# A four-layer sequence kernel on one core: the first attention of the next row in one stretch with the FFN of this row and the experts of the row before, without barriers between rows

## Time and profile before

| | us |
|---|---|
| median of 3 runs | 1578.21 |
| lowest and highest | 1576.48, 1590.58 |
| the profiled execution, its own time | 1577.19 |
| its span, first to last instruction | 1575.4 |
| busy in the span: TensorE | 1289.6 (82%) |
| VectorE | 851.7 (54%) |
| ScalarE | 666.1 (42%) |
| POOL | 107.2 (7%) |
| mean granted TensorE clock | 0.891 |

### The profile page before, as it was taken

The page is one execution under the profiler, slowest core; times in us unless marked ns, Lnnn a source line. Parts: engine busy times, 40 slices in busy tenths (PEclk is TensorE's granted clock), DMA queues, the critical chain, the costliest instruction groups (busy, mean ns, idle before and its releaser), DMA issues.

```text
span 1575.4 us, 19401 instructions
## 1 busy us (share of the span) xinstructions
PE 1289.6 (82%) x7257; PEld 643.8 (41%) x7257; DVE 851.7 (54%) x1816; ACT 666.1 (42%) x1407; POOL 107.2 (7%) x250
## 2 busy tenths in 40 slices
PE   2499458788898998788799899878789899878888
PEld 1122133445122564344322365444422267344556
DVE  6587446333785467433677365624578456633222
ACT  1067323352376442343166542254157643235232
POOL 4000001020000000020000000003000000000000
PEclk6599769799799999889699999889989999879989
DMA  7400000030000000030000000030000000000000
GB/s 149 111 2 2 8 0 1 21 41 2 1 2 2 1 7 1 1 61 9 2 2 2 1 7 1 1 61 2 7 1 2 1 1 1 1 1 1 8 1 8
DMA packets 31731, 21.04 MB, mean 13 GB/s; under 512 B 12873, under 2 KB 29329, under 8 KB 31633
## 3 DMA queue, kind: packets, MB, share of 16 engines
q1 hardware_dynamic: 31632, 19.75, 6.3%
HBM read 14.96 MB, written 4.19 MB: 12 GB/s over the span
## 4 chain that ended last, share of the span: by engine, by line
PE 64%; DVE 18%; ACT 7%; SPq 4%; issue 3%; DMA 2%; POOL 0%; DVEq 0%; POOLq 0%; PEldq 0%; ACTq 0%; another core or an unknown queue 0%
PE ps L1210 8%; PE ps L1142 8%; PE ps L1152 7%; DVE mx L726 6%; PE ps L1177 6%; PE ps L1291 6%; PE ps L1312 5%; PE ps L1185 5%; PE ps L1281 4%; ACT ps L1038 3%; PE ps L1324 3%; DVE mx L843 2%; DVE SH L817 2%; PE ps L1384 2%; ACT PROB L981 2%
## 5 line engine op out<-in xcount | busy, mean ns | idle before, releaser
L981 ACT ACTIVATE PROB<-ps 128x512 f32<-128x512 f32 x512 | 272.4, 606 | 284.0 <-PE ps L1177 283.9
L726 DVE TENSOR_REDUCE mx<-ps 128x1 f32<-128x512 f32 x512 | 318.7, 683 | 86.0 <-PE ps L1185 85.9
L1185 PE MATMUL ps<-KPAD,SH 128*128 128x512 bf16 x512 | 193.8, 431 | 54.9 <-SPq L352 35.0
L1038 ACT ACTIVATE ps<-ps,mx 128x128 f32<-128x128 f32 (+3 forms) x256 | 127.1, 497 | 252.6 <-DVE mx L843 252.6
L1312 PE MATMUL ps<-KPAD,SH 64*128 64x384 f32 (+3 forms) x512 | 171.4, 530 | 58.4 <-ACT ps L1038 50.2
L843 DVE TENSOR_REDUCE mx<-ps 128x1 f32<-128x128 f32 (+3 forms) x256 | 113.6, 486 | 189.8 <-PE ps L1315 189.8
L1177 PE MATMUL ps<-SH,KPAD 128*128 128x512 bf16 x512 | 163.3, 395 | 15.2 <-ACT PROB L981 9.9
L1291 PE MATMUL ps<-SH,KPAD 64*128 64x256 f32 (+3 forms) x512 | 139.5, 536 | 40.1 <-DMA m1row<-mrow 22.9
L1210 PE MATMUL ps<-PROB,v 128*32 128x512 f32 x1024 | 138.0, 614 | 6.8 <-ACT SH L972 4.7
L959 ACT ACTIVATE KPAD<-ps,b_sb 128x512 f32<-128x512 f32 x128 | 87.9, 687 | 126.8 <-PE ps L1142 126.4
L1312 PEld LDWEIGHTS ps<-KPAD,SH 64*128 64x128 f32 x512 | 79.9, 219 | 117.7 <-ACT ps L1038 98.2
(11 more groups left out here) (175 smaller groups left out, 1361.9 us busy)
## 6 DMA issues: line engine op xcount, KB each, us to landing
SH<-qk_parts SPq DMA_DIRECT2D x48, 128.0 KB, 6.4
qk_parts<-SH SPq DMA_DIRECT2D x8, 384.0 KB, 2.9
w_sb<-in_L_ffn_W_dram SPq DMA_DIRECT2D x1, 2048.0 KB
XN<-in_L_attn_x_dram SPq DMA_DIRECT2D x4, 256.0 KB, 2.9
out_dram<-XP SPq DMA_DIRECT2D x4, 256.0 KB, 2.3
wq_sb<-in_L_attn_Wq_dram SPq DMA_DIRECT2D x1, 512.0 KB, 5.4
rope_sb<-in_rope_dram SPq DMA_DIRECT2D x1, 512.0 KB
wo_sb<-in_L_attn_Wo_dram SPq DMA_DIRECT2D x1, 512.0 KB
```

The lines of the kernel that those rows point to most:

```text
L726: dve.tensor_reduce(mx[:, ga % 2, r % 16:r % 16 + 1], ps[:, 3 + r % 3, :], AX, ALU.max, negate=True).then_inc(max0_done, 1)
L981: act.activation(prob0[:, n % 2, c, k], ps[:, q % 3, :], ACT.Exp, scale=float(HD0) ** -0.5).then_inc(exp0_done, 1)
L1038: act.activation(tile, tile, ACT.Exp, bias=mx[:, (s + 1) % 2, col:col + 1], accum_out=lsum[:, (s + 1) % 2, 0, col:col + 1]).then_inc(sum1_ ...
L1185: pe.matmul(ps[:, 3 + r % 3, :], qst[:, a // 8, P * qt:P * (qt + 1)], kpad[:, a // 8, j, :], start=True, stop=True).then_inc(a0_ready, 1)
```

## The change

The loop over rows becomes an unrolled alternation of two stretches, the same on every engine: `overlap(-1)`, `attention1(-1)`, `overlap(0)`, `attention1(0)`, ..., `attention1(3)`, `overlap(4)`.

- `overlap(r)` goes through the 88 slots with first attention of row r + 1, the first FFN of row r (`ffn_stream`) and the experts of row r - 1 (`experts_stream`), whichever exist. `overlap(-1)` has first attention alone, `overlap(0)` no experts, `overlap(3)` no first attention, `overlap(4)` the experts of row 3 alone.
- `attention1(r)` is second attention of row r. In it stand the outputs, sum, norm and block scales of first attention of row r + 1, and turning, projecting and splitting x of row r + 2. `attention1(-1)` has only these.
- Semaphores count on through the rows; barriers and clearing are gone. Each row's output leaves by its own wait.
- Terms lie in 32-row strips: 24 rows of terms and 3 of maxima for each of the four head halves of a group (`M_ROW` is 24). A score or maximum uses one strip of `kst` and `qst`, `kpad` and its masked copies are gone. The terms are laid out on the way to DRAM: 12 stores for 2, 8 loads for 12. The row of maxima takes three transfers a group for one. POOL's per-row memsets of `kst` and `qst` are gone.
- PSUM: scores of first attention have 2 banks for 3 (0, 1), maxima and their turned rows share 2 (2, 3), values bank 4, experts 5 and 6, FFN 6 and 7. Experts have one hidden buffer, up products use banks 5 and 6, down products bank 6. In second attention maxima have 4 banks (2 to 5), scores one pair (0, 1).
- Rotary sums, the last four passes of both quantisations and the bias of the output are on POOL. Square roots (`std_b`, and of the RMS norm) stand between the exponentials of second attention (slots (0, 4) and (1, 4)) and of first attention (7, 2).

The core of the diff; the streams of VectorE and ScalarE follow the same tables of slots:

```diff
...
-A1_BANK = (4, 5, 7)
 
...
+A_LEAD = 13
+STEPS = [(s, c) for s in range(-4, 18) for c in range(4)]
...
+GATE_UP = {(-4, 0): 0, (-4, 2): 1, (-3, 0): 2, (-3, 2): 3}
+SILU = {(-4, 1): 0, (-4, 3): 1, (-3, 1): 2, (-3, 3): 3}
+HID_TURN = {(3, 0): 0, (4, 0): 1, (5, 0): 2, (6, 0): 3}
+HID_KEEP = {(3, 1): 0, (4, 1): 1, (5, 1): 2, (6, 1): 3}
+DOWN = {(3, 2): 0, (4, 2): 1, (5, 2): 2, (6, 2): 3}
+DOWN_KEEP = {(3, 3): 0, (4, 3): 1, (5, 3): 2, (6, 3): 3}
+O0_TURN = {(9, 0): 0, (9, 2): 1, (10, 0): 2, (10, 2): 3, (11, 3): 4, (13, 3): 5, (15, 3): 6, (17, 3): 7}
+O0_OUT = {(2 * g + 3, 0): g for g in range(NG)}
+UP = {(2 * e - 1, f): (e, f) for e in range(NE) for f in range(4)}
+OUT = {(2 * e, t): (e, t) for e in range(NE) for t in range(NT)}
+COMBINE = {(2 * e + 1, 0): e for e in range(NE)}
...
+def qk_banks(i):
+    return (0, 1) if i % 2 == 0 else (6, 7)
+
+
+def a1_bank(i):
+    return 2 + i % 4
...
+            def store_parts(k):
+                if k:
+                    sp.wait_ge(terms_in, 16 * 2 * HF * k)
+                for c, part in enumerate((Q_PART, K_PART)):
+                    sp.wait_ge(parts_ready, 2 * k + c + 1)
                     for t in range(NTERM):
-                        src = parts_dram[1 - c, part[t]].rearrange("(g r) n -> r g n", g=NG)
-                        sp.dma_start(dst[16 * t:16 * t + 16], src).then_inc(terms_in, 16)
...
+                        dst = terms_dram[c, t].rearrange("d j g n -> (j g) d n")
+                        sp.dma_start(dst, split[:, c, part[t]]).then_inc(parts_out, 16)
+                sp.wait_ge(parts_out, 16 * 2 * NTERM * (k + 1))
+
+            def load_terms(k):
+                if k:
+                    sp.wait_ge(av0_done, 16 * k)
+                for c, dst in ((1, kst), (0, qst)):
+                    for j in range(HF):
+                        src = terms_dram[c].rearrange("t d j g n -> j (t d) g n")[j]
+                        sp.dma_start(dst[32 * j:32 * j + M_ROW], src).then_inc(terms_in, 16)
...
+                    sp.wait_ge(slot0_free, SLOTS * k + ROW_SLOT[g] + 1)
+                    for i in range(3):
+                        sp.dma_start(qst[M_ROW + i::32, g, :], mrow0[16 * i:16 * i + 16, :]).then_inc(max0_in, 16)
+                    sp.wait_ge(max0_in, 48 * (NG * k + g + 1))
...
-                sp.wait_ge(row_ended, len(row_opened))
-                sp.sem_clear(row_ended)
-                clear(late)
-                for opened in row_opened:
-                    sp.sem_inc(opened, 1)
-
-            def body(row, first, last):
...
+            def rope_sum(r, i):
+                pool.wait_ge(rope_ready, 24 * r + 2 * (i + 1))
+                d = QK_ORDER[i]
+                dst = qT[:, d] if d < 8 else k1[:, d - 8]
+                pool.tensor_tensor(dst, ropeT[:, i % 2, 0], ropeT[:, i % 2, 1], ALU.add).then_inc(qk_ready, 1)
+
+            def quantise(a, c, n, done):
+
+                nb = n // QB
+                blk = lambda t: t.rearrange("p (b q) -> p b q", q=QB)
+                wide = lambda t: t.rearrange("p (b a) -> p b a", a=1).broadcast_to([P, nb, QB])
+                step(pool.tensor_scalar(c, c, 1.0, 1.5 * 2.0 ** 22, ALU.max, ALU.mult)); settle()
+                step(pool.tensor_tensor(a, a, c, ALU.add)); settle()
+                yield
+                step(pool.tensor_tensor(a, a, c, ALU.subtract)); settle()
+                pool.tensor_tensor(blk(a), blk(a), wide(q_sc[:, 0, 0:nb]), ALU.mult).then_inc(done, 1)
+                yield
...
+            def overlap(r):
+                k = r + 1
+                hidden = 0 <= r < BATCH
+                if hidden:
+                    pool.wait_ge(hs_ready, r + 1)
+                    rounds = quantise(ha, hc, 1408, hq_ready)
...
+                    if hidden and g < 2:
+                        next(rounds)
+                    if k < BATCH:
+                        max_parts0(k, g)
...
+                    if g == 2 and k < BATCH:
+                        pool.wait_ge(xs_ready, k + 1)
+                        for _ in quantise(XQ[:, :], ZB[:, :, :].rearrange("p t n -> p (t n)"), T, xq_ready):
+                            pass
+                    if g == 3 and nx < BATCH:
+                        split_next(nx, 0)
+                        split_next(nx, 1)
...
+                if (s, c) in UP:
+                    e, f = UP[s, c]
+                    if (e, f) == (0, 0):
+                        pe.wait_ge(ohT_ready, i + 1)
+                    if (e, f) == (0, 1) and i + 1 < BATCH:
+                        pe.wait_ge(hid_done, NT * (i + 2))
+                    if f == 1 and e:
+                        pe.wait_ge(comb_done, NT * (NE * i + e))
+                    if f >= 2 or e:
+                        pe.wait_ge(relu_done, 32 * i + 4 * e + f - 1)
+                    pe.matmul(ps[:, 5 + f % 2, :], w1_sb[:, e, P * f:P * (f + 1)], xnT[:, :], start=True, stop=True).then_inc(up_ready, 1)
+                if (s, c) in OUT:
+                    e, t = OUT[s, c]
+                    if t == 0:
+                        pe.wait_ge(relu_done, 32 * i + 4 * (e + 1))
+                    for f in range(4):
+                        ins = pe.matmul(ps[:, 6, P * t:P * (t + 1)], hE[:, f, P * t:P * (t + 1)], w2_sb[:, e, f, :],
+                                        start=(f == 0), stop=(f == 3))
+                    if t == NT - 1:
+                        ins.then_inc(down1, 1)
...
+                    if t == 0:
+                        pe.wait_ge(xT_ready, 2 * r + 1)
+                    else:
+                        pe.wait_ge(hid_done, NT * r + t)
+                    for u in range(2):
+                        ins = pe.matmul(ps[:, 6 + u, 0:FF0], xT[:, P * t:P * (t + 1)], wgT[:, u, :], start=True, stop=True)
+                    ins.then_inc(gu_ready, 1)
...
+            def overlap(r):
+                k, i = r + 1, r - 1
+                for s, c in STEPS:
+                    if k < BATCH:
+                        if 0 <= s < 16:
+                            g = s // 2
+                            if c == 0 and s % 2 == 0:
+                                pe.wait_ge(max0_in, 48 * (NG * k + g + 1))
+                            for q in (8 * s + 2 * c, 8 * s + 2 * c + 1):
+                                j, kt = q % 4, 2 * (s % 2) + q % 8 // 4
+                                rows = slice(32 * j, 32 * j + M_ROW + 3)
+                                if 128 * k + q >= 2:
+                                    pe.wait_ge(exp0_done, 128 * k + q - 1)
+                                pe.matmul(ps[:, q % 2, :], kst[rows, g, P * kt:P * (kt + 1)], qst[rows, g, :],
                                           start=True, stop=True).then_inc(s0_ready, 1)
-                        if 0 <= a < HF * 2 * NG:
-                            for u in range(2):
-                                r = 2 * a + u
-                                j, qt = r % 16 // 4, r % 4
-                                if r >= 3:
-                                    pe.wait_ge(max0_done, r - 2)
-                                pe.matmul(ps[:, 3 + r % 3, :], qst[:, a // 8, P * qt:P * (qt + 1)], kpad[:, a // 8, j, :],
-                                               start=True, stop=True).then_inc(a0_ready, 1)
...
+                        for n in maxima_at(s, c):
+                            j, qt, at = n % 4, n % 16 // 4, SLOTS * k + MAX_SLOT[n]
+                            rows = slice(32 * j, 32 * j + M_ROW)
+                            if n == 0:
+                                pe.wait_ge(terms_in, 16 * 2 * HF * (k + 1))
+                            if at >= 2:
+                                pe.wait_ge(slot0_free, at - 1)
+                            pe.matmul(ps[:, 2 + at % 2, :], qst[rows, n // 16, P * qt:P * (qt + 1)], kst[rows, n // 16, :],
+                                      start=True, stop=True).then_inc(slot0_full, 1)
+                        for g in max_rows_at(s, c):
+                            at = SLOTS * k + ROW_SLOT[g]
+                            pe.wait_ge(parts0_ready, NG * k + g + 1)
+                            pe.wait_ge(slot0_free, at - 1)
+                            pe.transpose(ps[:, 2 + at % 2, :].bitcast(BF16)[0:48, 0:P], mparts0[:, g % 2], identb).then_inc(slot0_full, 1)
+                    if 0 <= r < BATCH:
+                        ffn_stream(s, c, r)
+                    if 0 <= i < BATCH:
+                        experts_stream(s, c, i)
...
+                def turn(s, c):
+
+                    if k < BATCH and (s, c) == (1, 3):
+                        pe.wait_ge(on_ready, NT * (k + 1))
+                        for t in range(NT):
+                            ins = pe.matmul(ps[:, 7, P * t:P * (t + 1)], on[:, 2 * t:2 * t + 2].rearrange("p d h q -> p (d h q)"),
+                                            wo0_sb[:, :], start=True, stop=True)
+                        ins.then_inc(y0_ready, 1)
+                    if nx < BATCH:
+                        if (s, c) == (2, 1):
```

(14 more changed lines are left out.)

1565 lines of the change are left out of this document (681 added, 884 removed).

## The result

The changed kernel took 1752.59 us (median; 1750.04 to 1756.36) against 1577.35 for the kernel before on the same chip: ratio 1.107, 95% interval 1.103 to 1.111. The forecast was 1592 and its range ended at 1650. The profiled span is 1750.3 us, at a mean granted TensorE clock of 0.804 (0.891 before), as a share of the full 2.4 GHz.

What follows compares the result with a forecast made beforehand. In a middle row TensorE and the hand-overs to it were taken to set the pace. Terms -14 - 8 + 12 + 0 + 33 + 10 - 18 = +15 on 1577.2 gave about 1592 us, range 1515 to 1650.

Steps and rivals of the forecast that it cites:

- first scores begin: Start of kernel: without key copies and barrier, scores start near 61.5 instead of 76 us, -14; only -5 if DMAs queue.
- chain from row 0's values to row 1's max: After row 0's first attention: outputs, norm and sum 12 us, then fetch to stored terms 36, 48 before row 1's maximum.
- overlap(0), FFN beside it: Merged stretch without experts: lead-in 31, 16 groups 100, FFN 8, drain 4, so 143 us against 126.
- full stretches, each: Merged stretches of rows 1 and 2: lead-in 46, groups of 9.2, 204 us against 204, change 0 (-30 to +15).
- overlap(3), overlap(4): Last two rows: row 3's FFN with row 2's experts 110 us against 77, +33; final experts 81.4 before, +10.
- second attention, four rows: Second attention, 159 us a row before: -2 for rows 0 and 1, -6 row 2, -8 row 3, -18 in all.
- both signs that it named for being wrong: Groups with experts not near 9.2 us, or the last two stretches together not adding about 40 us.
- the 0.45 us that I took for them: Merged slots: cost of four bf16 score and maximum matmuls on four 32-row strips, between 0.25 and 0.97 us.
- Rival 1: Concurrency wins: strips overlap fully, lead-ins shrink to 40, groups 7.6, two stretches at 174 us, 1532 in all; chance 0.36.
- rival 2: Slot chain wins: two banks, four streams in order, groups 10.2 us, second attention 5 more a row, 1642; chance 0.17.
- The table loads, +4 a row: Second attention: two square roots amid exponentials cost at least four table loads of 1.28 us, +4 (0 to +8).
- a fourth bank for maxima: -6: Second attention: a fourth maxima bank attacks 9.3 us that TensorE waits for ScalarE, -6 us.

Runs made afterwards that it cites:

- f1: Kernel before the change, with ScalarE's exponential of a slot's scores ahead of that slot's maxima's sums in second attention: 1588.82 us, ratio 0.997 to the unedited one.
- b1: Changed kernel with second attention's scores alternating between two bank pairs, and two banks instead of four for maxima of the second to fourth head groups: 1717.40 us.
- a1: Changed kernel with ScalarE's exponential of a slot's scores issued ahead of the sums of that slot's maxima in second attention: 1607.09 us, ratio 1.017 to the kernel before.
- a2: Changed kernel with the two square roots in each second attention computed as exponential of half a logarithm, and one more table preload: 1728.86 us.
- d2: Changed kernel with exponential ahead of the sums in second attention and its square roots as exponential of half a logarithm: 1604.93 us, ratio 1.013 to the kernel before.
- d3: Changed kernel with exponential first, square roots by logarithm, two score bank pairs in second attention and two maxima banks from the second head group: 1714.58 us.
- c1: Changed kernel with three unused 128-row matmuls at each of 64 score steps in both first attentions without experts: 1750.89 us.
- c2: Changed kernel with three unused matmuls on rows 0 to 31 alone at each score step of the first attentions without experts: 1866.00 us.
- c4: Changed kernel with two unused 128-row matmuls only in the steps without a value product of the first attentions without experts: 1715.76 us.
- c3: Changed kernel with a third bank for the scores of the first attentions without experts, no added matmuls: 1729.69 us.
- f2: Changed kernel with exponential first, two unused 128-row matmuls in steps without value product, and a third score bank in overlap(-1): 1565.53 us, ratio 0.988 to the kernel before.

## Why the prediction was wrong

Step by step, forecast against the changed kernel:

```
step                                       forecast    measured
first scores begin                          61.5         61.3
chain from row 0's values to row 1's max    48           47.9
first attention of row 0                    101 (as before)  134.4
overlap(0), FFN beside it                   143         168.4
full stretches, each                        204         201.6, 201.7
  lead-in and slots of one                  46, 158       50.8, 150.8
  one group of them                         9.2           9.4
overlap(3), overlap(4)                      110, 91      106, 97
second attention, four rows                 618         732
```

618 is 4 x 159 - 18; 732 is 187.7 + 187.5 + 184.1 + 172.8. The group of 9.4 is the mean of the first fifteen in 650.5:790.9 and has the FFN's slots in it, for which the forecast had 8 us apart; the middle one of them takes 9.05. The misses, +33, +25, -5, -4, +6 and +114, make 169, against 161 between forecast and median. No rival of the prediction reached that far (the highest was 1642), and both signs that it named for being wrong stayed silent: the groups came near 9.2, and the last two stretches took 203 us where they had taken 158, 45 more where about 40 was named. They watched the parts that were right.

**Right:** the start, the chain through fetch, projection, split and terms, the full stretches as a sum (their two parts miss by 5 and 7 us and cancel, which is luck), and the last two. The four strips overlap, so the 0.45 us that I took for them was about the 0.4 of the trace. Rival 1 expected groups of 7.6 from that, and rival 2 groups of 10.2 from the banks; both were wrong, as the group is 9.4.

**The step that failed most** is in second attention (forecast 618 us for the four rows, measured 732), the sentence "Scores have one bank pair instead of two, so six times a row the exponential of 1.02 is exposed; moved products fill some: +4." It took the exponential's own duration as the price. I counted banks and durations and did not lay the two engines' programs side by side: TensorE has scores, then maxima; ScalarE has the maxima's sums, then the exponential. With two pairs this order is harmless (f1, and the wait of 4.9 us in b1), with one it puts everything in a line (a1). In the slot shown the exponential starts 4.4 us after its scores are there, from 842.7 to 847.07, and TensorE stands for 2.83 us. In all TensorE waited 51 times for it, 13 times a row and not six, for 117.1 us, and it paid nearly as much again in clock (in the row measured, 18.3 us to 22.5). With the order mended there are 20 waits of 27.7 us, five a row and 7 us, which is near the six of 1.02 in the sentence: it had priced another order of instructions. Rival 2 named the right place, with 5 us a row. Second attention of row 0, mended, is 412:561.2, 149 us, where I had forecast 157. The table loads, +4 a row or 16 in all, cost 24 (a2), and most of that hung on the same order (d2).

The step "a fourth bank for maxima: -6" is not settled. TensorE's wait for the sums is 50.2 us in the kernel before with three banks and 31.7 in the changed kernel with four, 5 a row less, but more than the bank differs between them. d3 shows that two are too few by 110 us; no run of the changed kernel has three.

**The other step** was silent: first attention without experts was given the slots of the kernel before, 100 us for the 16 groups, and those ran at 0.97 and 0.98 with scores and maxima on all 128 rows. Strips of 24 and 27 rows and value products leave the granted clock at 0.62 though TensorE is busy for 119.8 of 134.4 us. c1 and c2 show that it is the rows in use: the same number of extra matmuls gives 0.95 on 128 rows and 0.53 on 32. c4 shows that the time follows: 109.7 us at 0.90. The waits for two banks are tied up with it: a third bank gives 14 us of this stretch at the low clock (c3) and 3.4 at the high one (f2), where it takes 107.0 us, against 100 in the kernel before. I had set a fear that the strips are not concurrent against a hope that they are, and never asked what clock such a stretch gets when the experts aren't beside it.

The Trainium skill's rule that I weighed (TensorEngine Tiling, Key Properties: a change of tiling mode drains the array) shows no large price: at 700.11 to 704 scores in strips, down products, up products and values follow one another at once, and the slots came 7 us under the forecast that took 0.1 us a change. That strips start some 4 ns apart (the Trainium skill, TensorE: Matmul & The Clock Gate, Part 3) agrees with the trace as far as its 10 ns steps tell: 703.16 and 703.17.

## What to carry to other kernels

When a change takes away a second buffer, write down the order of both engines' programs around the one that is left: an instruction that is needed early but stands behind others that wait for later work costs their whole chain, and a swap of two blocks may give it back (-145.5 us here). Price a slimmer form of matmul at the clock that the stretch will get with it: if it leaves most rows of the array unused, as the 24 and 27 rows here did, work the sum out at the durations of 1.2 GHz too, and try a few matmuls of 128 rows in steps where TensorE waits anyway. A small cost measured in a kernel with a large wait in it (24 us of table loads) or at a low clock (14 for a third bank) may be nearly gone once that is mended.

## What the runs showed that was not expected

- Matmuls on 32 rows, TensorE busy for 97% of a stretch: clock 0.53. The same on 128 rows: 0.95, and the kernel's time as without them (1750.9). Work without use can pay if it stands where the engine waits: 128 of these 128-row matmuls in two stretches gave -36.8 us.
- A wait lowers the clock for what follows (1.00 before and 0.50 after the 2.83 us in which TensorE did nothing from 845.3): second attention at 0.80 with TensorE busy for 102.35 us, at 0.94 for 84.02 once most waits were gone, the same instructions.
- Four matmuls on different 32-row strips, 512 columns each, in 0.40 us together (703.16 to 703.56) at full clock and 0.62 (122.89 to 123.51) at half.
- Function tables, as they were put in for ScalarE: with a square root between exponentials and logarithms the changed kernel loads 24 tables more than the logarithm form with its one preload more (56 against 32). After it exponentials and logarithms each get a table of their own, as on the changed kernel's timeline:

```profile
512.77 1.28 ACT L953 ACT_TABLE_LOAD   x1
514.07 0.22 ACT L953 ACTIVATE lsum<-lsum 128x16 f32<-128x16 f32 x1
514.30 1.28 ACT L966 ACT_TABLE_LOAD   x1
515.60 1.02 ACT L966 ACTIVATE PROB<-ps 128x1024 f32<-128x1024 f32 x1
```
